# A two-layer transformer block: the first experts in two token batches, the second batch routed inside the experts' stage

## The chip, the core and the metric

One core of a Trainium2 chip. Its engines run side by side, each with its own instruction stream, and meet only through semaphores: PE (matmul, with PEld for its weight loads), DVE (elementwise and reductions), ACT (activation functions), POOL (elementwise, and the indirect DMAs that send and gather rows) and SP (which does nothing but read registers and issue DMAs). The metric is the device time of one execution in microseconds (us). Before the change its median of three runs is 1006.11 us (1004.85 to 1008.36).

## The reference

x is (128, 64, 128) in fp32: 8192 tokens of 128 values, here 64 tiles of 128 tokens, or 32 groups of two tiles. Four sublayers follow one another, each added to x after a layer norm:

```python
x = x + cross_attention_0(norm(x), ctx, ctx, padding)   # 16 heads of 8, causal, exact softmax
x = x + moe_0(norm(x))                                  # 16 experts, top 2
x = x + cross_attention_1(norm(x), ctx)                 # 2 heads of 64
x = x + moe_1(norm(x))                                  # 8 experts, top 1, and a shared expert
```

The sublayer that the change turns about is moe_0. Written as the kernel computes it, with xt the normed tokens:

```python
logits = xt @ Wr + br                       # 16 logits a token
w, idx = top_k(softmax(logits), 2); w /= w.sum()
h = gelu(xt @ W1[e] + b1[e])                # 128 -> 256, for the token's two experts e
y = xt + sum(w[e] * (h @ W2[e] + b2[e]) for e in idx)
```

Here the sublayer itself adds xt (the normed rows) as well.

## The kernel before

The program is a row of stages, each a block in which every engine has its own program; a stage begins when all engines have ended the one before. The stages are `opening`, `layer0_attention`, `experts` (with gated=False), `layer1_attention`, `route_and_share` and `experts` again (gated=True). x stays in SBUF (`x_sb` in the trace) from the beginning to the end.

`opening` (L67) loads x in four quarters on SP (L94), the small weights on ACT's queue, and behind x, on SP too, eight later loads (L96): the weights of the second attention and of the routers. The first attention begins when SP has issued them.

`layer0_attention` (L205) works in steps i, one group of two tiles a step: scores, softmax over four large DVE operations (L389 is the first of them), transposes, output, sum into x (L419). SP loads the context of each group (L276) into two buffers. Three steps behind (LATE = 3) the group is normed a second time (L377, into `f_xn_all`), transposed (L648), and multiplied with the router (L671); DVE keeps the logits (L412), finds the best two (`best_of`, L1194), and for chunks of 8 tiles (at the end, of 4) chooses and counts: matmuls give every token its rank within its expert (L1162, L1164), and `places` turns ranks to row numbers. POOL then sends each tile's rows to their experts' regions in DRAM, two indirect DMAs a tile (`send`, L1155). So steps 0 to 31 do attention, steps 3 to 34 routing, and the tail finishes the last chunks. SP loads, after the last context, 32 pieces of expert weights (L1117, L1120), then writes zeros: one spare region (L1138), 15 spare pieces of the output (L1141), and, when the counts are known, behind each expert's last row one block (`blank_rows`, L1132; SP takes eight experts and ACT eight; four row numbers at a time are read into registers). DVE computes from the counts which slot works on which expert and rows (`starts`, then `slots_by_partition` and `outs_by_partition`), PE turns that table (L686), and DVE keeps it.

`experts` (L1474) walks 80 slots: 64 pairs of 256 rows and 16 singles of 128 rows. In slot J SP loads the rows (L1540, four buffers, the row number from a register; a table of four is read at a time), PE transposes them (L1677), ACT copies, PE multiplies with W1 (L1694), ACT applies gelu (L1664), PE multiplies with W2 (L1704), DVE adds the bias (L1614, the slot's result) and copies the weights of the expert two slots ahead (L1587). POOL stores the result (L1560), again from a table of row numbers, and beside it sums x with the normed rows (L1563), 32 times in all. In the singles DVE also computes from where each token's two results are to be fetched (L1624 to L1630). PE's order in a slot is turn(J + 1), W1 of J, W2 of J - 1; PE works its instructions in order.

`layer1_attention` (L690) lets POOL gather for each tile the two result rows of each token (L758, 128 indirect DMAs in all, into a ring of buffers), DVE weights and adds them to x (L771), norms (L796), and PE begins with L948. PE, ACT and DVE walk the groups in hardware loops.

Of the kernel before, what the change touches and what calls it, by code (L numbers as in the profile page):

```python
# [37 lines left out]
X_CHUNKS = 4  # L38

# [27 lines left out]
def opening(nc, A, R):  # L67
    n = TILES // X_CHUNKS
    with ExitStack() as ctx:
# [4 lines left out]
        R.later_loaded = sem("later_loaded")  # L74
# [9 lines left out]
        for tag, (wr, br) in R.router.items():  # L84
            later += [(wr[:, :], A[tag + "_wr"]), (br[:, :], A[tag + "_br"].partition_broadcast(P))]
        R.later = len(later)
# [118 lines left out]
def layer0_attention(nc, A, R, N):  # L205

    NT, NG, E = TILES, GROUPS, N.experts
    CHUNKS = [8] * 6 + [4] * 4
# [3 lines left out]
    RANKED = [i + 2 if i < NG else i + 1 for i in CHOOSES]  # L212
    PLACES = [i + 1 if i < NG else i for i in RANKED]
    LAST = NG + LATE
    assert FIRST[-1] == NT
# [10 lines left out]
    with ExitStack() as ctx:  # L226
# [4 lines left out]
        ctxT = sb("ctxT", [P, 2, GT])  # L231
# [7 lines left out]
        K = Ranks(nc, ctx, A, R, N, max(CHUNKS))  # L239
# [19 lines left out]
        st0_done, slots_done, table_ready = sem("st0_done"), sem("slots_done"), sem("table_ready")  # L259
        xn_ready, xb_done, xk_done, xnT_ready, kx_ready = (sem(n) for n in ("xn_ready", "xb_done", "xk_done", "xnT_ready", "kx_ready"))  # L260
# [10 lines left out]
        def _(sp):  # L271
# [13 lines left out]
            K.clear_tails(sp, R.zeros[:, :, :], N.experts // 2)  # L285

        @block.gpsimd
        def _(pool):
# [31 lines left out]
            def body(p, k, low):  # L320
# [3 lines left out]
                if k == 1 and low >= 1 and within(i - LATE, NG):  # L324
                    inverse(p - 1)

            LAST_INVERSE, sent = NG + 1, 0
            for i in range(LAST_INVERSE + 1):
                placed = [FIRST[c + 1] for c in range(len(CHUNKS)) if PLACES[c] < i]
                tiles = min(2 if i < 24 else 3, max(placed, default=0) - sent)  # L330
                if i == LAST_INVERSE:
                    at_hand = max(FIRST[c + 1] for c in range(len(CHUNKS)) if PLACES[c] < NG)
                    for t in range(sent, at_hand + 1):
                        K.send(pool, max(c for c in range(len(CHUNKS)) if FIRST[c] <= t), t, t + 1)
                    sent, tiles = at_hand + 1, 0
                if i <= LAST_INVERSE:
                    body(i // 2, i % 2, i // 2)
                for n, t in enumerate(range(sent, sent + tiles)):
                    if n < 2 and within(i, NG):
                        pool.wait_ge(mx_done, 2 * i + n + 1)  # L340
                    K.send(pool, max(c for c in range(len(CHUNKS)) if FIRST[c] <= t), t, t + 1)
                sent += tiles
            for t in range(sent, TILES):
                K.send(pool, max(c for c in range(len(CHUNKS)) if FIRST[c] <= t), t, t + 1)
            pool.wait_ge(K.sent, 16 * TILES * N.top)

        @block.vector
        def _(dve):
# [84 lines left out]
            def body(p, k, low):  # L433
                i = 2 * p + k
                scored, added = within(i, NG), within(i - 1, NG)
                routed = 2 * low + k >= LATE and within(i - LATE, NG)
                if within(i + 2, NG):
                    norm(i + 2)
                if within(i - 2, NG):
                    statistics(i - 2, k)  # L440
# [7 lines left out]
                if routed and i <= NG + 1:  # L448
                    second_norm(i - LATE, p - 2 + k, k)
                if i == NG + 1:  # L450
                    second_norm(NG - 1, p - 1, 0)
# [5 lines left out]
                if LATE < i <= NG + LATE:  # L457
# [5 lines left out]
                for c in range(len(CHUNKS)):  # L463
                    if PLACES[c] == i != RANKED[c]:
                        K.places(dve, c, FIRST[c], CHUNKS[c])
                    if PLACES[c] == i == RANKED[c] and added:
                        K.positions(dve, rank_ps, c, FIRST[c], CHUNKS[c])
# [4 lines left out]
                for c in range(len(CHUNKS)):  # L472
                    if PLACES[c] != i == RANKED[c]:
                        K.read_ranks(dve, rank_ps, c, CHUNKS[c])
                    if PLACES[c] == i == RANKED[c] and not added:
                        K.positions(dve, rank_ps, c, FIRST[c], CHUNKS[c])
            passes(body)
            K.starts(dve)
            K.slots_by_partition(dve)
            K.outs_by_partition(dve)  # L480
            dve.sem_inc(slots_done, 1)
# [4 lines left out]
        def _(act):  # L486
# [39 lines left out]
            def body(p, k, low):  # L526
                i = 2 * p + k
                routed = 2 * low + k >= LATE and within(i - LATE, NG)
# [26 lines left out]
        def _(pe):  # L555
            def proj_xk(G, g, use):
                pe.wait_ge(loaded[g], 16 * (use + 1))
# [35 lines left out]
            def turn(i, u):  # L593

                pe.wait_ge(p_ready, 2 * i + u + 1)
                for half in range(2):
                    if u == 0 and half == 0 and needed(i - LATE + 1):
# [9 lines left out]
            def weighted(i, u, g):  # L607
# [3 lines left out]
                if u == 0 and needed(i + 1 - LATE):  # L611
# [15 lines left out]
            def body(p, k, low):  # L627
                i = 2 * p + k
                r = i - LATE
                routed = 2 * low + k >= LATE and within(r, NG)  # L630
                if within(i, NG):
                    scores(i, k)
                if i - 1 in RANKED and not within(i - 1, NG):
                    pe.wait_ge(K.read, RANKED.index(i - 1) + 1)
# [22 lines left out]
                if routed:  # L657
# [8 lines left out]
                    else:  # L666
                        pe.wait_ge(x_done, NG)
                    if i in RANKED and i in PLACES and within(i - 1, NG):
# [375 lines left out]

# [768 lines left out]
```

## Time and profile before

| | us |
|---|---|
| median of 3 runs | 1006.11 (1004.85 to 1008.36) |
| the profiled execution | 1005.86 |
| its span in the trace | 1004.0 |
| PE busy in the span | 821.1 (82%) |
| DVE busy | 666.0 (66%) |
| ACT busy | 578.2 (58%) |
| POOL busy | 511.1 (51%) |
| opening until the next stage's first instruction | 17.16 |
| first transpose of the experts | 400.44 |
| last result of the experts | 550.26 |
| first matmul of the second attention | 573.29 |

A busy share is the mean over stages that have different limits, so it is read by stage: the windows view gives for a stretch the busy time of each engine, the granted clock of TensorE as a share of full speed (PEclk) and the DMA engines' share. In a timeline, the brackets behind a row hold the idle time of its engine before it and the instruction that released it. SPq, POOLq, PEq and so on are the queues of the engines (DMA issues and signals); "issue" means that nothing in the trace explains the wait.

### The profile page before, as it was taken

How to read it: one execution, taken by the hardware profiler on the slowest of the kernel's cores; microseconds unless marked ns; L12 is line 12 of the kernel's file. 1: busy time of each engine (PE TensorE's matmuls, PEld its weight loads, DVE VectorE, ACT ScalarE, POOL GpSimd, SP SyncE). 2: the span in 40 equal slices, each digit the busy share in tenths (PEclk: the TensorE clock that was granted, in tenths of full speed). 3: DMA queues.
4: the chain of work that ended last, by engine and by line, in shares of the span. 5: the costliest groups of instructions: out<-in, count | busy, mean ns of one | idle time of the engine just before them, and what ended most of it. 6: DMA issues, size and time to landing. Idle time of an engine off the chain costs nothing. (4 is left out here: it accounts for less than half of the span.)

```text
span 1004.0 us, 27974 instructions
## 1 busy us (share of the span) xinstructions
PE 821.1 (82%) x9234; PEld 689.1 (69%) x9234; DVE 666.0 (66%) x2294; ACT 578.2 (58%) x1339; POOL 511.1 (51%) x612
## 2 busy tenths in 40 slices
PE   0699999999999820999998178888858998959997
PEld 0478877878777710999997055555547887849996
DVE  3788899999989742344446379999963546425554
ACT  0588888888888500666665177777756551213332
POOL 4011145555564765344445677777400644726777
PEclk9799999999999855999999599999998999979999
DMA  6000011111116413344332233333213213244441
GB/s 206 11 19 18 14 39 37 47 44 40 49 40 194 143 45 101 112 135 136 131 125 94 72 83 78 82 82 79 55 31 124 85 67 118 107 137 141 145 122 55
DMA packets 67572, 86.33 MB, mean 86 GB/s; under 512 B 22000, under 2 KB 50037, under 8 KB 66960
## 3 DMA queue, kind: packets, MB, share of 16 engines
q1 hardware_dynamic: 47728, 44.71, 15.2%
q0 software_dynamic: 17152, 39.36, 12.1%
q10 hardware_dynamic: 2592, 0.95, 0.5%
q8 instruction: 60, 0.98, 0.4%
q14 instruction: 40, 0.33, 0.1%
HBM read 50.47 MB, written 35.01 MB: 85 GB/s over the span
## 5 line engine op out<-in xcount | busy, mean ns | idle before, releaser
L1155 POOL DMA_INDIRECT f_rows_in<-f_xn_all,f_pos_i x128 | 126.1, 985 | 68.5 <-DVE a_mx L389 34.4
L758 POOL DMA_INDIRECT a_got<-f_rows_out,f_pos_i x128 | 122.7, 958 | 41.5 <-issue 35.4
L1155 POOL DMA_INDIRECT f_rows_in<-f1r_xn_all,f_pos_i x64 | 61.6, 962 | 70.8 <-DVEq L1222 31.3
L1552 POOL DMA_INDIRECT out<-f1e_y,f1e_ids x72 | 76.5, 1062 | 41.3 <-DVE f1e_y L1611 24.7
L1560 POOL DMA_DIRECT2D f_rows_out<-f0e_y x80 | 43.8, 547 | 88.3 <-DVE f0e_y L1614 71.4
L1664 ACT ACTIVATE f0e_hT<-f0e_ps_h,f0e_w 128x256 f32<-128x256 f32 (+1 forms) x160 | 63.8, 449 | 38.5 <-PE f0e_ps_h L1694 38.5
L1614 DVE TENSOR_TENSOR f0e_y<-f0e_ps_y,f0e_w 128x256 f32<-128x256 f32 (+1 forms) x80 | 31.7, 397 | 80.9 <-PE f0e_ps_y L1704 80.6
L618 PE MATMUL a_ps_o<-vx,a_prT 128*64 128x18 f32 x2048 | 83.6, 215 | 2.0 <-DVE x_sb L419 2.0
L618 PEld LDWEIGHTS a_ps_o<-vx,a_prT 128*64 128x64 f32 x2048 | 79.7, 140 | 7.7 <-issue 4.7
L293 POOL TENSOR_TENSOR x_sb<-x_sb,bo 128x256 f32<-128x256 f32 x32 | 23.3, 727 | 116.3 <-DVE a_xn L354 116.0
L389 DVE TENSOR_REDUCE a_mx<-a_ps_s 128x16 f32<-128x1024 f32 x64 | 77.7, 1215 | 5.1 <-PE a_ps_s L589 4.9
L512 ACT ACTIVATE a_pr<-a_pr,sharp 128x1024 f32<-128x1024 f32 x64 | 74.1, 1158 | 10.0 <-DVE a_pr L397 9.4
L1694 PE MATMUL f0e_ps_h<-f0e_xT,f0e_w 128*128 128x256 f32 (+1 forms) x320 | 77.9, 367 | 2.2 <-ACT f0e_xT L1646 1.8
L397 DVE TENSOR_TENSOR a_pr<-a_ps_s,a_mx 128x1024 f32<-128x1024 f32 x64 | 77.9, 1216 | 1.7
L604 PE MATMUL a_ps_t<-ident,a_pr 128*128 128x128 f32 x512 | 71.4, 281 | 9.0 <-ACT a_xnT L542 5.3
L1704 PEld LDWEIGHTS f0e_ps_y<-f0e_w,f0e_hT 128*128 128x128 f32 x576 | 76.0, 192 | 3.8 <-ACT f0e_hT L1664 0.4
L1704 PE MATMUL f0e_ps_y<-f0e_w,f0e_hT 128*128 128x128 f32 x576 | 77.8, 276 | 0.2 <-ACT f0e_hT L1664 0.2
L519 ACT ACTIVATE a_prT<-a_ps_t 128x512 f32<-128x512 f32 x128 | 69.4, 594 | 14.6 <-PE a_ps_t L604 14.4
L604 PEld LDWEIGHTS a_ps_t<-ident,a_pr 128*128 128x128 f32 x512 | 55.4, 142 | 29.1 <-issue 14.1
L1694 PE MATMUL f1e_ps_h<-f1e_xT,f1e_w 128*128 128x256 f32 (+1 forms) x320 | 70.2, 363 | 0.1
L490 ACT ACTIVATE a_kx<-a_ps_p,own_bk,own 128x256 f32<-128x256 f32 x128 | 65.8, 577 | 0.0
L1601 DVE TENSOR_TENSOR f1e_hT<-f1e_ps_h,f1e_hg 128x512 f32<-128x512 f32 (+1 forms) x40 | 25.5, 638 | 50.3 <-ACT f1e_hg L1659 41.9
(300 smaller groups left out, 2043.3 us busy)
## 6 DMA issues: line engine op xcount, KB each, us to landing
f1e_x<-f_rows_in SPq DMA_DIRECT2D x32, 272.0 KB, 2.7
a_ctxT<-in_ctxT SPq DMA_DIRECT2D x64, 128.0 KB, 2.1
f0e_x<-f_rows_in SPq DMA_DIRECT2D x64, 128.0 KB, 2.0
f_rows_out<-f0e_y POOLq DMA_DIRECT2D x64, 128.0 KB, 2.0
f_w<-in_f_w SPq DMA_DIRECT2D x16, 257.0 KB
x_sb<-in_x SPq DMA_DIRECT2D x4, 1024.0 KB, 5.0
f_w<-in_f_w SPq DMA_DIRECT2D x8, 384.0 KB, 6.4
f_rows_in<-f_xn_all,f_pos_i POOLq DMA_INDIRECT x128
```

Source lines behind the costliest of these rows:

```text
L389: dve.tensor_reduce(by_strip(mx[:, u, :]), scores(u), AX.X, ALU.max).then_inc(mx_done, 1)
L397: dve.tensor_tensor(pr[:, u, :, :].rearrange("p (s j) k -> p s j k", s=STRIPS), scores(u), peaks, ALU.subtract).then_inc(d_ready, 1)
L490: last = act.activation(kx[:, g, j, :], ps_p[:, GT:2 * GT], ACT.Identity, scale=R.own[:, j:j + 1], bias=R.own_bk[:, j:j + 1])
L512: act.activation(pr[:, u, :, :], pr[:, u, :, :], ACT.Exp, scale=R.sharp[:, bass.ds(2 * i + u, 1)]).then_inc(p_ready, 1)
L519: act.activation(prT[:, u, js, :], ps_t[:, js, :], ACT.Copy).then_inc(t_evac, 1)
L604: last = pe.transpose(ps_t[:, j, :], pr[:, u, 2 * j:2 * j + 2, :].rearrange("p h k -> p (h k)"), ident[:, :])
L618: last = pe.matmul(ps_o[rows, 144 * u + 18 * j:144 * u + 18 * j + 18], prT[:, u, j, rows], vx[:, g, 2 * u + b, j, :, :].rearrange("p e c - ...
L758: pool.indirect_dma_start(got[:, n, k, :], None, N.rows_out[0:N.most, :], bass.IndirectOffsetOnAxis(ap=N.pos_i[:, k, t:t + 1], axis=0)).th ...
L1155: pool.indirect_dma_start(N.rows_in, bass.IndirectOffsetOnAxis(ap=N.pos_i[:, k, t:t + 1], axis=0), self.xn_all[:, t, :], None).then_inc(se ...
L1552: pool.indirect_dma_start(rows_of_out, bass.IndirectOffsetOnAxis(ap=ids[:, n, u:u + 1], axis=0), y[:, n, u, :], None, bounds_check=B * S - ...
L1694: last = pe.matmul(ps_h[m][:, j, 0:size], w[:, n, j * P:(j + 1) * P], xT[:, m, 0:size], start=True, stop=True)
L1704: last = pe.matmul(ps_y[1 - m][:, u * P:(u + 1) * P], hT[:, 1 - m, j, u * P:(u + 1) * P], w[:, l, H + j * C:H + (j + 1) * C], start=(j == ...
```

## The change

The tokens are routed in two batches, tiles 0 to 47 and tiles 48 to 63, each with its own rows in DRAM, its own counts and its own slots.

- Opening: SP issues the context of groups 0 and 1 behind the first quarter of x, and the eight later loads move into the first attention's SP program, behind the loads of its first two groups there.
- First attention: only groups 0 to 23 are routed, in six chunks of 8 tiles; the blocks, starts and slots are computed in steps 30 to 32. POOL sends 48 tiles. SP writes the spare zeros of both batches (2 x 16 pieces) before the tail blanks.
- First experts: a stage of its own, `first_experts`, with all loops unrolled, for 64 slots of batch A (48 pairs, 16 singles) and 32 of batch B (16 pairs, 16 singles): 96 in all. SP issues both the loads and, six slots behind, the stores of the results. Groups 24 to 31 are normed, transposed and given logits in slots 11 to 20, chosen and ranked in 22 to 29, and their table is made in 31 to 41; POOL sends their rows. At slot 46 SP blanks batch B's sixteen tails. POOL first does the sums of x, then, after the sends and when all of A's results are stored, gathers the first 18 tiles for the second attention.
- Second attention: POOL gathers from tile 18 on, into a ring of 16 groups that lies where the normed rows were; DVE's loop is unrolled.
- The second experts keep their work, as `second_experts`.

```diff
@@ opening, SP
                 if c == 1:
+                    for g in range(2):
+                        sp.dma_start(R.ctxT[:, g, :], A["ctxT"][:, GT * g:GT * (g + 1)]).then_inc(R.ctx_first[g], 16)
                     sp.wait_ge(w_loaded, 16 * len(first))
                 sp.dma_start(R.x[:, tiles, :], R.xd[:, tiles, :]).then_inc(R.x_loaded[c], 16)
-            for place, data in later:
-                sp.dma_start(place, data).then_inc(R.later_loaded, 16)
@@ layer0_attention
-    CHUNKS = [8] * 6 + [4] * 4
+    EG = EARLY // 2
+    CHUNKS = [8] * (EARLY // 8)
-    LAST = NG + LATE
+    LAST = NG
@@ layer0_attention, SP
-            rounds(sp, body, NG // 2, last=0)
+            for place, data in R.later_loads:
+                sp.dma_start(place, data).then_inc(R.later_loaded, 16)
+            body(1)
+            with sp.Fori(2, NG // 2) as i:
+                body(i)
             K.load_weights(sp, shared=False)
             sp.wait_ge(R.later_loaded, 16 * R.later)
             sp.wait_ge(zeros_made, 1)
+            spares = sum(blank_spare(sp, N, batch, R.zeros[:, :, :], spare_blank) for batch in N.batches)
             K.clear_tails(sp, R.zeros[:, :, :], N.experts // 2)
+            sp.wait_ge(spare_blank, 16 * spares)
@@ first_experts, SP
+            for J in range(NS + LAG):
+                if J == BLANK_AT:
+                    K.clear_tails(sp, R.zeros[:, :, :], E)
+                if J == NA:
+                    sp.wait_ge(slots_kept, 1)
+                    sp.wait_ge(K.sent, 16 * 2 * BG * N.top)
+                if J < NS:
+                    Q, j = batch(J)
+                    if j % NB == 0:
+                        rows = table(Q.slot_row[0:1, j:j + NB], mybir.EngineType.SP, Q.spare)
+                    if J >= NB:
+                        sp.wait_ge(xT_done, J - NB + 1)
+                    sp.dma_start(x[:, J % NB, 0:wide(J), :],
+                                 Q.rows_in[bass.ds(rows[j % NB], wide(J) * P), :].rearrange("(p u) c -> p u c", p=P)).then_inc(loaded[J % NB], 16)
+                if J >= LAG:
+                    L = J - LAG
+                    Q, j = batch(L)
+                    if j % NB == 0:
+                        outs = table(Q.slot_out[0:1, j:j + NB], mybir.EngineType.SP, Q.last_out)
+                    sp.wait_ge(y_ready, L + 1)
+                    sp.dma_start(Q.rows_out[bass.ds(outs[j % NB], wide(L) * P), :].rearrange("(p u) c -> p u c", p=P),
+                                 y[:, L % NB, 0:wide(L), :]).then_inc(stored[L % NB], 16)
@@ first_experts, POOL
+            for G in range(EARLY // 2):
+                sum_norm(G)
+            pool.wait_ge(ag_done, 1)
+            pool.tensor_scalar(var[:, :], mv[:, :, 1], EPS, None, ALU.add).then_inc(var_ready, 1)
...
+            pool.tensor_tensor(rstd[:, :], var[:, :], half[:, :], ALU.pow).then_inc(rstd_ready, 1)
+            for v in range(BG):
+                pool.wait_ge(K.kept, v + 1)
+                sum_norm(EARLY // 2 + v)
+            for t in range(EARLY, TILES):
+                K.send(pool, 0, t, t + 1)
+            pool.wait_ge(K.sent, 16 * 2 * BG * N.top)
...
+            for n in range(NB):
+                pool.wait_ge(stored[n], 16 * (NA // NB))
+            for t in range(FETCHED):
+                gather(pool, N, t)
@@ first_experts, DVE, for each J
+                    result(J - 1)
...
+                    weights(ahead, e[j % NB])
...
+                if NORM_AT <= J < NORM_AT + BG:
+                    norm(J - NORM_AT)
+                if LOGITS_AT < J <= LOGITS_AT + BG:
+                    keep_logits(J - LOGITS_AT - 1)
@@ first_experts, PE, for each J, behind turn(J + 1), W1 of J and W2 of J - 1
+                if TURN_AT <= J < TURN_AT + BG:
+                    v = J - TURN_AT
+                    pe.wait_ge(K.kept, v + 1)
+                    if v > 0:
+                        pe.wait_ge(nT_ready, v)
+                    for u in range(2):
+                        last = pe.transpose(ps_n[:, u * P:(u + 1) * P], N.xn_all[:, EARLY + 2 * v + u, :], R.ident[:, :])
+                    last.then_inc(nT_done, 1)
+                if LOGITS_AT <= J < LOGITS_AT + BG:
+                    v = J - LOGITS_AT
+                    pe.wait_ge(nT_ready, v + 1)
+                    if v > 0:
+                        pe.wait_ge(l_ready, v)
+                    for u in range(2):
+                        last = pe.matmul(l_ps[:, u, :], late_T[:, u * P:(u + 1) * P], wr[:, :], start=True, stop=True)
+                    last.then_inc(l_done, 1)
+                if J == RANK_AT:
+                    K.rank_matmuls(pe, rank_ps, 0, LATER)
@@ layer1_attention
-        got = sb("got", [P, 2 * NB, K, C])
+        got = N.xn_all[:, :, :].rearrange("p (n k) c -> p n k c", k=K)
```

The constants of the new stage are EARLY = 48, FETCHED = 18, RING = 16, LAG = 6, NORM_AT = 11, TURN_AT = 12, LOGITS_AT = 13, BEST_AT = 22, RANK_AT = 27, READ_AT = 28, BLOCKS_AT = 31, TABLE_AT = 37, TURNED_AT = 40, KEPT_AT = 41 and BLANK_AT = 46; NB = 4 buffers each for x, w and y.

## Rows read from the trace of the kernel before

**Rows 1.** Windows of three stages: seam, pairs, second attention (start:end, length, busy, granted clock).

```profile
354.00:400.00 46.00, 5.60 (x29) 3.59 (x28) 17.45 (x104) 0.77 (x2) 29.37 (x32) 0.50 0.23 69
...
400.00:531.00 131.00, 130.41 (x906) 122.77 (x907) 56.39 (x130) 80.77 (x198) 57.73 (x94) 0.98 0.40 128
...
573.00:749.00 176.00, 140.29 (x1472) 97.77 (x1472) 148.42 (x617) 124.66 (x380) 108.49 (x114) 0.98 0.27 67
```

**Rows 2.** Timeline of the opening (start, duration, engine, line, operation, idle before and its releaser).

```profile
12.47 0.61 SPq L96 DMA_DIRECT2D w1wq<-in_a_wq  x1
...
16.20 0.49 SPq L96 DMA_DIRECT2D f_br<-in_f_br  x1
...
17.21 1.86 DVE L354 TENSOR_SCALAR a_xn<-x_sb,mean,rstd 128x128 f32<-128x128 f32 x1 [4.40 <-PEq L69]
...
23.10 0.47 PE L562 MATMUL a_ps_p<-ident,a_xn 128*128 128x128 f32 x1 [10.89 <-DMA a_ctxT<-in_ctxT]
```

**Rows 3.** Timeline of DVE: the first reduction of four steps of the first attention.

```profile
57.27 1.23 DVE L389 TENSOR_REDUCE a_mx<-a_ps_s 128x16 f32<-128x1024 f32 x1 [0.42 <-PE a_ps_s L589]
...
65.95 1.22 DVE L389 TENSOR_REDUCE a_mx<-a_ps_s 128x16 f32<-128x1024 f32 x1 [0.42 <-PE a_ps_s L589]
...
287.05 1.21 DVE L389 TENSOR_REDUCE a_mx<-a_ps_s 128x16 f32<-128x1024 f32 x1
...
334.41 1.21 DVE L389 TENSOR_REDUCE a_mx<-a_ps_s 128x16 f32<-128x1024 f32 x1
```

**Rows 4.** Timeline around the end of the first attention: SP's queue, POOL, PE.

```profile
310.41 0.33 SPq L276 DMA_DIRECT2D a_ctxT<-in_ctxT  x1
...
329.10 10.20 SPq L1141 DMA_DIRECT2D f_rows_out<-zeros  x15
...
379.07 0.33 SPq L1132 DMA_DIRECT2D f_rows_in<-zeros  x1
...
381.27 1.88 SPq L1132 DMA_DIRECT2D f_rows_in<-zeros  x4
...
394.14 0.96 POOL L1155 DMA_INDIRECT f_rows_in<-f_xn_all,f_pos_i  x1 [0.30 <-issue]
...
400.44 0.48 PE L1677 MATMUL f0e_ps_x<-ident,f0e_x 128*128 128x128 f32 x1 [16.16 <-DMA f0e_x<-f_rows_in]
```

**Rows 5.** Timeline of DVE in the experts: first pair, last pair, last single.

```profile
407.03 0.42 DVE L1614 TENSOR_TENSOR f0e_y<-f0e_ps_y,f0e_w 128x256 f32<-128x256 f32 x1 [6.43 <-PE f0e_ps_y L1704]
407.37 0.48 DVE L1587 COPY f0e_w<-f_w 128x642 f32 x1
...
531.16 0.43 DVE L1614 TENSOR_TENSOR f0e_y<-f0e_ps_y,f0e_w 128x256 f32<-128x256 f32 x1 [0.61 <-PE f0e_ps_y L1704]
...
550.26 0.29 DVE L1614 TENSOR_TENSOR f0e_y<-f0e_ps_y,f0e_w 128x128 f32<-128x128 f32 x1 [0.60 <-PE f0e_ps_y L1704]
```

**Rows 6.** The page's DMA issues (out<-in, queue, count, KB each, us to landing).

```profile
f0e_x<-f_rows_in SPq DMA_DIRECT2D x64, 128.0 KB, 2.0
```

**Rows 7.** Routing's operations by line (count: ns min/median/max, first and last start).

```profile
L648 PE MATMUL a_ps_t<-ident,f_xn_all x64: 272/273/477, 70.2 to 368.9; 128*128 128x128 f32 x64
...
L671 PE MATMUL a_ps_o<-f_wr,a_xnT x128: 182/262/395, 72.0 to 370.4; 128*128 128x16 f32 x128
...
L377 DVE TENSOR_SCALAR f_xn_all<-x_sb,a_mv,a_rstd x64: 329/341/568, 69.2 to 365.2; 128x128 f32<-128x128 f32 x64
```

**Rows 8.** POOL's sums in the experts and its powers in the first attention, by line.

```profile
L1563 POOL TENSOR_TENSOR x_sb<-x_sb,f_xn_all x32: 737/744/913, 410.7 to 532.8; - x28, 128x256 f32<-128x256 f32 x4
...
L302 POOL TENSOR_TENSOR a_rstd<-a_var,minus_half x16: 1037/1042/1048, 68.1 to 363.4; 128x4 f32<-128x4 f32 x16
```

**Rows 9.** The gathers of the second attention, who waited for them, and its first matmul.

```profile
L758 POOL DMA_INDIRECT a_got<-f_rows_out,f_pos_i x128: 940/947/1168, 554.6 to 715.0; - x128
...
  DVE x_sb L771: 9.7, 6
...
573.29 0.45 PE L948 MATMUL a_xk<-ident,a_xn 128*128 128x128 f32 x1 [23.07 <-DVE a_xn L796]
```

More of the change, by code:

```diff
@@ L38 @@
 X_CHUNKS = 4
+EARLY = 48
+FETCHED = 18
+RING = 16
 def needed(count):
@@ L462, in body @@
                     K.choose(dve, FIRST[c], CHUNKS[c])
[L463 to L467, printed above, removed]
+                if i in PLACES:
+                    c = PLACES.index(i)
+                    K.places(dve, c, FIRST[c], CHUNKS[c])
+                if i == NG - 2:
+                    K.blocks_by_expert(dve)
+                if i == NG - 1:
+                    K.starts(dve)
                 if added:
@@ L471, in body @@
                     keep_logits(i - LATE)
[L472 to L476, printed above, removed]
+                if i in RANKED:
+                    c = RANKED.index(i)
+                    K.read_ranks(dve, rank_ps, c, CHUNKS[c])
             passes(body)
[L478 to L481, printed above, removed]
             dve.wait_ge(table_ready, 1)
@@ L1040, in clear_stale, with __init__ @@
     R.stale = []
[L1043 to L1062 removed]
+class Batch:
+    def __init__(self, nc, sb, N, tag, first, tiles):
+        self.first, self.tiles, experts = first, tiles, N.experts
+        self.region = tiles * P + SLOT
+        self.pairs, self.singles = tiles * P * N.top // SLOT, experts
+        self.slots = self.pairs + self.singles
+        self.spare = experts * self.region
+        self.rows_in = nc.dram_tensor(f"{tag}_rows_in", (self.spare + SLOT, N.row), F32, kind="Internal").ap()
+        self.slot_e = sb(tag + "_slot_e", [P, LEAD + self.slots], I32)
+        self.slot_row = sb(tag + "_slot_row", [P, self.slots], I32)
+        if not N.final:
             self.sure, self.most = 2 * self.pairs * P, (2 * self.pairs + experts - 1) * P
@@ L1243, in starts @@
              dve.scalar_tensor_tensor(self.until[:, :], own[:, 0, :], float(SLOT), start[:, :], ALU.mult, ALU.add))
+    def starts(self, dve):
+        E, N, Q = self.N.experts, self.N, self.Q
+        step = lambda *instructions: self.step(dve, *instructions)
+        start, own, ends = self.start, self.own, self.ends
         a, b, d = own, self.sums, 1
@@ L1289, in keep_slots, with blank_spare @@
     def keep_slots(self, dve, turned):
-        N = self.N
-        dve.tensor_copy(N.slot_e[0:1, LEAD:], turned[:, 0:N.slots])
-        dve.tensor_copy(N.slot_row[0:1, :], turned[:, P:P + N.slots])
-        if not N.final:
-            dve.tensor_copy(N.slot_out[0:1, :], turned[:, 2 * P:2 * P + N.slots])
+        Q = self.Q
+        if not self.N.final:
+            dve.tensor_copy(Q.slot_out[0:1, :], turned[:, 2 * P:2 * P + Q.slots])
+        dve.tensor_copy(Q.slot_row[0:1, :], turned[:, P:P + Q.slots])
+        return dve.tensor_copy(Q.slot_e[0:1, LEAD:], turned[:, 0:Q.slots])
+def blank_spare(queue, N, Q, blank, done):
+    queue.dma_start(Q.rows_in[Q.spare:, :].rearrange("(p u) c -> p u c", p=P), blank).then_inc(done, 16)
+    if N.final:
+        return 1
+    for row in range(Q.sure, Q.most, P):
+        queue.dma_start(Q.rows_out[row:row + P, :], blank[:, 0, :]).then_inc(done, 16)
+    return 1 + (Q.most - Q.sure) // P
 def route_and_share(nc, A, R, N):
@@ L1534, in body @@
             def body(i):
-                rows = table(N.slot_row[0:1, bass.ds(NB * i, NB)], NB, mybir.EngineType.SP, N.spare)
+                rows = table(Q.slot_row[0:1, bass.ds(NB * i, NB)], NB, mybir.EngineType.SP, Q.spare)
                 for n in range(NB):
```

539 lines of the change are left out of this document (348 added, 191 removed).

## The prediction

> **What bounds the kernel now.** I read the stage windows first, then the waits, then the timelines at the seams between stages. The first experts run on a full PE: busy 130.4 of 131 us [rows 1]. The seam before them is nearly empty: of 46 us PE works 5.6 and DVE 17.5 [rows 1]. The change buys time at three seams (opening, routing tail, start of the second attention) and pays for it inside the stage that has no idle PE. So there are two columns: what the seams give, and what the experts' stage grows by.
>
> The profiled execution took 1005.86 us (span 1004.0, the rest lies around it), 0.25 below the median of 1006.11, so what I take off or add to one holds for the other.
>
> **A, opening: -7.7.** The next stage starts at 17.21 with a norm, because SP still issues its eight later loads, the first at 12.47, the last at 16.20 [rows 2]. PE then starts at 23.10, released by the context DMA, which queues behind x [rows 2]. With both edits the stage starts when DVE's opening ends, about 13.3 (some 0.5 after SP's x loads are issued, 12.47). The first norm takes 1.86 us [rows 2], so PE starts near 15.3, 7.8 earlier; I count 7.7 for a slightly late quarter of x. The eight loads still cost SP about 4.2 us, now beside a step of about 8.7; nobody waits for them before the blanking, and SP has done its context loads of that step. Bounds: 0 (if what is late next is the rest of x, whose statistics DVE takes right behind) and 9.
>
> **B and C, the end of the first attention: together with A -47.** A step with no routing lasts 65.95 - 57.27 = 8.68; the last five average (334.41 - 287.05)/5 = 9.47 [rows 3]. Routing now ends with group 23, three steps late, so five steps lose 0.8 each. Then the tail: today POOL's last send ends at 394.14 + 0.96 = 395.10 and the experts' first transpose is at 400.44, 5.3 later [rows 4]. With 96 sends, up to three tiles a step, the sends end a few us after the last step begins (334.41 - 7.7 - 4.0 = 322.7), near 340. So what is late next? SP. Its program is: last context load (310.41 today; less 7.7 and two shortened steps, 301.1); 32 weight loads and the first spare blank, after which it stands at 329.10 today, 18.7 later, so at 319.8; then the other spare blanks, 15 today in 10.20 us, 0.68 each [rows 4], 31 now, 21.1: 340.9. Then eight tail blanks behind two register tables: a blank every 0.52 (four in 1.88), a table between 379.07 and 381.27 adds 2.20 - 0.52 = 1.68 [rows 4], so 8 x 0.52 + 2 x 1.68 = 7.5: 348.4. Plus the same 5.3 for landing, barrier and first load: 353.7 instead of 400.44, -47. Bounds: -53 if the spare blanks go at 0.5 each, -40 if the sends or the last output set the end.
>
> **D, 96 slots for 80, and SP carries stores: +28.** A pair takes (531.16 - 407.03)/63 = 1.97 us, a single (550.26 - 531.16)/16 = 1.19 [rows 5]. Sixteen more singles at that rate: +19. But SP now issues a load and a store per slot and reads two register tables per four slots: 8 x 0.52 + 2 x 1.68 = 7.5 by the rows of the blanking; where a table's read lies partly beside a wait, less (I estimate down to 1.1 a table, 6.4). I take 7.0 for four slots, 1.74 a slot. That hides under a pair (1.97), not under a single. SP starts a run of singles about four or five slots ahead and needs one or two for the landing of 2.0 us [rows 6]; with 2.5 slots to use up, n singles go at 1.19 until 1.19 n = 1.74 (n - 2.5), n = 8. So 8 x 1.19 + 8 x 1.74 = 23.5 for each sixteen, twice 47, less 19.1 = +28. Bounds +19 (SP hidden) and +36 (no lead). *The Trainium skill's page DMA: Bandwidth & Descriptors (Issuing engines are not separate DMA queues) holds that issuing from several engines saves only sequencer time, which is usually small beside the DMA. By that, giving the stores to SP costs nothing, D is +19 and the sum 1017; the rows of SP show why I don't follow it here: issue and table together are near the length of a slot.*
>
> **E, routing's PE work: +9.** Eight times two transposes (0.273 each) and four logit records (0.262 each) [rows 7] are 1.6 us end to end, about half where they overlap: 6.4 to 12.8. With 17 or more rank records of that kind and the slot table, 9 (7 to 16). PE has no idle time in the pairs, so this is on the path.
>
> **F, waits that routing adds: +25.** In slots 14 to 20 PE's logits of group v wait for DVE's reading of group v-1, since both use one piece of PSUM, and DVE reads only after that slot's result: y_done, result 0.42, weights 0.48 [rows 5], the norms of two tiles at 0.341 each [rows 7], then the reading itself, a smaller operation than the result; some 0.2 with its signals, my estimate. That is 1.7 us in which PE holds its next slot's matmuls behind the logits in order. 7 x 1.65, and one or two of these slots also hold DVE's register table: 13.6. The norm at slot 11 waits for POOL: 24 sums of 0.744 are 17.9 us, then a power over 128x16 [rows 8], which the trace shows only at 128x4, 1.04 us: between 1.04 and 4.2, I take 2. Slot 11 comes at about 23 us (cold first slots, row 407.03 is 6.6 after the first transpose), so this costs 0 to 6, I take 3. Choosing, ranks and reading (slots 22 to 28) are a round trip DVE, PE, DVE of some ten short operations, and PE's rank matmuls stand in order behind the choice; starts and slots (29 to 41) are longer chains of such operations, with only the slot table waited for by PE. DVE's lead of two slots, 3.9 us, hides what is shorter than that: between 0 and 12 for all, and I take 8.5, nearer the upper end, since the logits' slots have used up that lead. Bounds for F: +8 (only one short wait in each logits slot) and +32.
>
> **G, blanking at slot 46: +15.** SP stops its loads and stores for 16 blanks and four tables, 16 x 0.52 + 4 x 1.68 = 15.0, waits for them to land (2.0) and then loads slot 46, which takes 0.5 and 2.0 [rows 4, 6]: 19.5. It begins when SP is four slots ahead of PE, worth 4 x 1.97 = 7.9 less what SP waits for that slot's result, about 7. PE stands 12.4; the results stand too, because stores of slots 40 to 43 are behind the blanks and y has four buffers. Today's stage also shows the granted clock at 0.50 after an empty stretch [rows 1]; a pause of 12 us can cost 2 to 3 more. Bounds: +6 (lead of six slots and faster blanks) and +18.
>
> The stage grows by 28 + 9 + 25 + 15 = **+77**.
>
> **H, second attention: -9.4.** Its first matmul is at 573.29 after 23.07 idle; DVE waited 9.7 us in six waits for gathers issued from 554.55 on, (715.0 - 554.6)/127 = 1.26 us apart [rows 9]. 18 tiles (36 gathers, 45 us) now go beside batch B's slots (16 x 1.97 + 23.5 = 55 us), after all of A's stores, and so end in time. Later gathers: 4 x 1.26 = 5.0 per group of two tiles, against 176/32 = 5.5 for a group of this stage [rows 1], with nine groups of lead: not late. Bounds 0 and -10. DVE's unrolled loop and the second experts: 0, between -2 and +2.
>
> **Sum:** 1005.9 - 47 + 77 - 9.4 = 1026.5; forecast **1026 us, slower**. Its own range is 1012 to 1042, from the bounds of F, G and D taken together.
>
> **Rivals.**
> *PE stays fed (other side).* Four x and y buffers and a lead of two slots cover the logits round trips and most of the blanking. Then only D and E are left, +28 to +37, and F and G give 0 to 12: 1005.9 - 47 + 37 - 9.4 = 986, range 970 to 1003. For it: DVE is busy for 0.42 + 0.48 of each 1.97 in the pairs [rows 5], and a small operation finds room. Against: PE works in order, and the logits stand between two slots' matmuls. It decides where F and G together stay below 19.4 of my 40.
> *SP bounds all slots.* If an issue with its waits takes 0.6 and a table 1.7, a slot is 2.05 for pairs too: 64 x 0.08 + 16 x 0.3 = +10 on the sum, 1036. Against: 64 slots have a slack of 0.2.
> *Half clock inside the stage.* The stretch 354 to 400 had 0.50 [rows 1]. If the thinned slots 11 to 28 or those after the blanking run at 1.2 GHz, some 10 us of PE work count twice: 1038.
> *The early gathers come late.* If B's slots pass faster than 45 us, or gathers wait for A's last stores, H is lost: 1035. Here the change would not do what it says at that seam.
> *Nothing measurable.* F and G at half: 1006.
>
> **How the numbers follow.** Forecast 0.42, PE fed 0.24, SP 0.09, clock 0.10, late gathers 0.08, no difference 0.07. A run of this kernel tells about 3 us (0.3%) from nothing. So faster 0.24, same 0.07, slower 0.69. Range **985 to 1042**: half of the fast rival and the top of the clock's lie outside.
>
> **What would show it.** The first transpose of the experts near 353.7, with SP's blanks as the last releaser (if POOL's sends or the last output are, C's steps are wrong). PE idle before the logits' line in seven slots, released by DVE; one idle of some 12 us before the transpose of slot 46, released by DMA. Results of the later singles 1.7 apart. The second attention's first matmul some 13 us after the experts' last result, not 22.7. If the stage from first transpose to last result is below 206 us instead of 227, I am wrong on the sign, and the idle times before these two lines say which of F and G it was.

## The result: 3.5% slower, and the profile after

The changed kernel takes 1042.45 us (median of four runs, 1037.80 to 1045.56) against 1005.48 for the kernel before on the same chip; the ratio is 1.0349, with a 95% interval of 1.0315 to 1.0383. The forecast was slower, 1026, in a range of 985 to 1042, so the median lies just above its upper end. The sign was right; some 15 us of the experts' stage were missing from the sum.

The profiled execution is the fastest of the four (1037.80, span 1036.0), so the terms below add up to +32 of the median's +37. The other three, which left no trace, show a mean granted clock of 0.935 to 0.946 against 0.952, and their 5 us stay open.

The windows of the changed kernel, with the columns of [rows 1]: the seam behind the last output of the first attention, then A's pairs, A's singles, B's pairs, B's singles.

```profile
339.00:349.30 10.30, 0.81 (x4) 0.22 (x2) 1.45 (x5) 0.00 (x0) 2.65 (x5) 0.50 0.45 120
349.30:502.00 152.70, 115.87 (x751) 104.72 (x752) 66.58 (x268) 63.18 (x157) 56.15 (x63) 0.92 0.34 103
502.00:529.80 27.80, 19.25 (x149) 17.14 (x149) 14.63 (x39) 14.10 (x48) 0.00 (x0) 1.00 0.30 85
529.80:565.60 35.80, 31.84 (x224) 29.48 (x223) 14.80 (x38) 19.34 (x49) 23.25 (x23) 1.00 0.55 156
565.60:591.20 25.60, 20.07 (x138) 18.79 (x136) 10.61 (x31) 12.69 (x44) 12.86 (x13) 0.87 0.41 111
```

The seam of 46 us [rows 1] is 10 us now. In return PE, which was busy in 130.4 of 131 us, stands for 37 of the 153 us of A's pairs.

The granted clock of TensorE has a smaller part in it. In the stage of before it is at full speed (2.4 GHz) from 406.5 on; here it falls to half (1.2 GHz) six times behind the first slots. The first four lines are from A's pairs, the last two from B's singles:

```profile
390.30:393.70 3.40, 2.87 (x13) 2.33 (x11) 0.92 (x3) 0.93 (x3) 0.00 (x0) 0.51 0.14 39
434.80:438.20 3.40, 3.24 (x21) 2.92 (x22) 0.84 (x3) 0.38 (x1) 0.00 (x0) 0.51 0.18 60
448.40:451.80 3.40, 3.40 (x15) 3.13 (x14) 1.58 (x11) 1.12 (x3) 2.48 (x4) 0.50 0.53 163
485.40:495.70 10.30, 5.11 (x18) 4.64 (x19) 0.83 (x2) 1.60 (x4) 0.25 (x1) 0.53 0.34 100
571.20:574.50 3.30, 3.30 (x18) 3.30 (x18) 1.15 (x4) 1.77 (x6) 2.62 (x3) 0.51 0.50 134
584.90:588.40 3.50, 3.50 (x19) 3.50 (x18) 1.07 (x5) 1.60 (x6) 0.00 (x0) 0.51 0.30 84
```

PE is busy for 21.4 us in them. Four W1 products take 1.92 us at half clock (491.07, shown under e4) and 1.03 at full clock, so I estimate that about half of the 21.4 is due to the clock: some 7 us in A's pairs and 3 in B's singles. Each fall comes during or soon after a wait of PE, but other waits (3.39 us until 409.05) bring none, and no run changes the clock alone.

The timelines of the changed kernel at the places of [rows 2], [rows 4] and [rows 9]: PE's first matmul, SP's and ACT's last blanks, the experts' first transpose and last result, the second attention's first matmul.

```profile
14.88 0.66 PE L570 MATMUL a_ps_p<-ident,a_xn 128*128 128x128 f32 x2 [3.08 <-DVE a_xn L361]
...
327.79 8.37 SPq L1305 DMA_DIRECT2D f0b_rows_out<-zeros  x15
337.96 5.47 SPq L1137 DMA_DIRECT2D f0b_rows_in<-zeros  x8
338.48 5.29 ACTq L1137 DMA_DIRECT2D f0b_rows_in<-zeros  x8
349.36 0.48 PE L1748 MATMUL f0e_ps_x<-ident,f0e_x 128*128 128x128 f32 x1 [9.55 <-DMA f0e_x<-f0b_rows_in]
...
591.17 0.29 DVE L1618 TENSOR_TENSOR f0e_y<-f0e_ps_y,f0e_w 128x128 f32<-128x128 f32 x1 [0.60 <-PE f0e_ps_y L1756]
603.57 0.66 PE L951 MATMUL a_xk<-ident,a_xn 128*128 128x128 f32 x2 [12.44 <-DVE a_xn L800]
```

| part | forecast | measured on the profiled execution |
|---|---|---|
| A, B, C: first transpose of the experts | -47 | 349.36 - 400.44 = -51.1 |
| D to G: experts, first transpose to last result | +77 | (591.17 - 349.36) - (550.26 - 400.44) = +92.0 |
| H: last result to the next first matmul | -9.4 | 12.40 - 23.03 = -10.6 |
| the rest | 0 | (1036.0 - 603.57) - (1004.0 - 573.29) = +1.7 |
| sum | +20.6 | +32.0 |

So three of the four rows came out within some 4 us, and the stage's row is the one that was missed. What PE waited for in that stage, as the waits view of the changed kernel groups it (total, times, longest):

```profile
PE f0e_ps_x L1748 <- DMA f0e_x<-f0b_rows_in: 25.7, 9, 9.5
PE f0e_ps_h L1772 <- issue: 13.1, 8, 2.4
PE f0e_ps_r L1793 <- DVE f0r_logits L1643: 12.8, 7, 3.4
PE f0e_ps_h L1772 <- ACT f0e_xT L1720: 9.5, 11, 1.2
PE f0e_ps_r L1159 <- DVE f0r_chosen L1201: 3.0, 1, 3.0
```

Three of these were forecast: the seven waits for logits (L1793), the wait for ranks (L1159), and the blanking, which is 8.9 of the first line (another 9.5 of it is the stage's start, and 7.3 are waits for the rows of singles). The two lines of L1772, PE's first product with W1, were not: nineteen waits and 22.6 us, of which 12.1 fall in A's pairs, 4.0 in B's pairs and 6.6 in the singles. The profile names ACT's xT or nothing at all for them. DVE's and PE's timelines in one such slot show what is behind it:

```profile
356.75 0.42 DVE L1618 TENSOR_TENSOR f0e_y<-f0e_ps_y,f0e_w 128x256 f32<-128x256 f32 x1 [0.27 <-PE f0e_ps_y L1756]
359.09 0.66 DVE L1609 COPY f0e_w<-f_w 128x642 f32 x1 [1.92 <-PE f0e_ps_y L1756]
...
359.85 1.10 PE L1772 MATMUL f0e_ps_h<-f0e_xT,f0e_w 128*128 128x256 f32 x4 [0.95 <-ACT f0e_xT L1720]
```

The matmul starts 0.10 after the copy of its weights ends (359.09 + 0.66 = 359.75); ACT had been done since 358.94 + 0.38 = 359.32. And the copy starts 1.92 after the result, though in other slots it follows at once [rows 5]. Between the two DVE reads the numbers of the next four experts into registers; such instructions are not counted as busy, so no row shows them. In the code of before this read stands at the head of the four slots, ahead of the wait for the first result; in the change it stands behind the result.

### The profile page after: what moved, and what is told of

Its sections match the earlier page's. It is cut to its first block and busy times, and to the rows that moved or that the text cites. A ratio compares the mean times of both kernels' runs of the same rounds, so it can differ in the third digit from the quotient of the medians.

```text
span 1036.0 us, 27913 instructions
## 1 busy us (share of the span) xinstructions
PE 851.1 (82%) x9381; PEld 713.7 (69%) x9381; DVE 679.4 (66%) x2352; ACT 590.8 (57%) x1387; POOL 466.7 (45%) x526
## 5 line engine op out<-in xcount | busy, mean ns | idle before, releaser
L1152 POOL DMA_INDIRECT f0b_rows_in<-f_xn_all,f_pos_i x128 | 125.9, 983 | 103.2 <-DVE a_mx L396 37.2
L694 POOL DMA_INDIRECT f_xn_all<-f0b_rows_out,f_got_i x128 | 124.1, 970 | 100.8 <-DMA f0b_rows_out<-f0e_y 49.8
L1731 ACT ACTIVATE f0e_hT<-f0e_ps_h,f0e_w 128x256 f32<-128x256 f32 (+1 forms) x192 | 73.6, 434 | 66.7 <-PE f0e_ps_h L1772 66.5
L1772 PE MATMUL f0e_ps_h<-f0e_xT,f0e_w 128*128 128x256 f32 (+1 forms) x384 | 92.4, 366 | 22.6 <-issue 13.1
L1878 POOL DMA_INDIRECT out<-f1e_y,f1e_ids x72 | 76.6, 1064 | 42.7 <-DVE f1e_y L1917 27.6
L1152 POOL DMA_INDIRECT f1b_rows_in<-f1r_xn_all,f_pos_i x64 | 61.4, 959 | 71.2 <-DVEq L1219 31.5
L1756 PE MATMUL f0e_ps_y<-f0e_w,f0e_hT 128*128 128x128 f32 x640 | 91.5, 284 | 0.2 <-ACT f0e_hT L1731 0.2
L1756 PEld LDWEIGHTS f0e_ps_y<-f0e_w,f0e_hT 128*128 128x128 f32 x640 | 88.3, 200 | 4.0 <-ACT f0e_hT L1731 0.4
L1772 PEld LDWEIGHTS f0e_ps_h<-f0e_xT,f0e_w 128*128 128x128 f32 x384 | 64.4, 203 | 30.7 <-issue 14.7
L1609 DVE COPY f0e_w<-f_w 128x642 f32 x96 | 50.2, 525 | 53.2 <-issue 36.7
L1720 ACT ACTIVATE f0e_xT<-f0e_ps_x 128x256 f32<-128x256 f32 (+1 forms) x96 | 33.4, 348 | 58.0 <-PE f0e_ps_x L1748 57.5
```

What stands on the lines that cost most here:

```text
L694: pool.indirect_dma_start(N.xn_all[:, N.top * place + k, :], None, Q.rows_out[0:Q.most, :], bass.IndirectOffsetOnAxis(ap=N.got_i[:, k, t:t ...
L1152: pool.indirect_dma_start(Q.rows_in, bass.IndirectOffsetOnAxis(ap=N.pos_i[:, k, t:t + 1], axis=0), self.xn_all[:, t, :], None).then_inc(se ...
L1731: last = act.activation(hT[:, m, j, 0:size], ps_h[m][:, j, 0:size], ACT.Gelu, bias=w[:, J % NB, B1 + j:B1 + j + 1])
L1756: last = pe.matmul(ps_y[m][:, u * P:(u + 1) * P], hT[:, m, j, u * P:(u + 1) * P], w[:, n, H + j * C:H + (j + 1) * C], start=(j == 0), stop ...
L1772: last = pe.matmul(ps_h[m][:, j, 0:size], w[:, n, j * P:(j + 1) * P], xT[:, m, 0:size], start=True, stop=True)
L1878: pool.indirect_dma_start(rows_of_out, bass.IndirectOffsetOnAxis(ap=ids[:, n, u:u + 1], axis=0), y[:, n, u, :], None, bounds_check=B * S - ...
```

## The experiments

Each ran against the kernel before; "less" and "more" are differences of ratios, times 1006. The changed kernel is at 1.0349. Most ratios are known to 0.002 or 0.003 either way, so a difference of two of them to some 4 us.

**e1, the opening alone** (kernel before, with only the edits of the opening).

```diff
+                    for g in range(2):
+                        sp.dma_start(R.ctxT[:, g, :], A["ctxT"][:, GT * g:GT * (g + 1)]).then_inc(R.ctx_first[g], 16)
...
-            for place, data in later:          # in opening; now in layer0_attention, behind its first loads
...
```

> The kernel before with the opening's two edits alone (context of groups 0 and 1 behind the first quarter of x, the eight later loads in the next stage). My theory (term A): everything behind the opening moves up with the first matmul, -7 to -9 us, about 997.5. Rival: only the first matmul moves, and the statistics that DVE takes of the last quarter of x hold the first step, so 0 to -3 us.

0.9911 (0.9889 to 0.9934), 999.24 us: 9 us less than before. Its first matmul is at 15.24 instead of 23.10 [rows 2], and its first softmax reduction at 30.17 instead of 38.0. Term A holds, and x's last quarter does not delay the first step.

**e2, the register table ahead of the result.**

```diff
             for J in range(-LEAD, NS + 1):
-                if 0 < J:
-                    result(J - 1)
                 ahead = J + LEAD
                 if ahead < NS:
...
                     if j % NB == 0:
                         e = table(Q.slot_e[0:1, LEAD + j:LEAD + j + NB], mybir.EngineType.DVE, E - 1)
+                if 0 < J:
+                    result(J - 1)
+                if ahead < NS:
                     weights(ahead, e[j % NB])
```

> The changed kernel, with DVE reading its register table of the next four experts ahead of the slot's result (while it waits for PE anyway) instead of behind it. Theory: the idle times of PE before its first W1 matmul, 1.0 to 2.7 us in every fourth slot, are this table, which stands between the result and the copy of the next weights: 14.6 us in batch A's pairs, 4 more in the two logit slots that hold a table, and some 5 to 11 in batch B and the singles, so -15 to -25 us, about 1020. Rival: these waits are the fetching of the unrolled program or a busy SBUF port; then the order of the two changes nothing, 1038 to 1045.

1.0195 (1.0165 to 1.0225): 15.5 us less than the changed kernel. DVE's timeline of e2 at a slot with a table:

```profile
365.41 0.42 DVE L1618 TENSOR_TENSOR f0e_y<-f0e_ps_y,f0e_w 128x256 f32<-128x256 f32 x1 [0.70 <-PE f0e_ps_y L1757]
365.75 0.48 DVE L1609 COPY f0e_w<-f_w 128x642 f32 x1
```

The copy follows the result at once, and the waits of PE at its W1 product fall from 22.6 to 9.2 in e2. The place of the table was the cause, not the fetching of the unrolled program. Of the 9.2, 8.6 are four waits that stay, in slots 11, 31, 35 and 39 (7.6 in the changed kernel). There DVE comes late from its routing work and has no wait in which the read could hide; its idle time now stands before the result:

```profile
436.32 0.17 DVE L1218 CAST f_pos_i<-f_pos 128x16 int32<-128x16 f32 x1
438.82 0.42 DVE L1618 TENSOR_TENSOR f0e_y<-f0e_ps_y,f0e_w 128x256 f32<-128x256 f32 x1 [2.33 <-issue]
```

**e10, the same order in the kernel before.** The opposite test: only the place of this read is changed, in the hardware loop of before.

```diff
-                if ahead > 0:
+                if gated and ahead > 0:
                     e = table(N.slot_e[...], ahead, mybir.EngineType.DVE, N.experts - 1)
...
+                    if n == 0 and not gated and ahead > 0:      # behind the result of slot J - 1
+                        e = table(N.slot_e[...], ahead, mybir.EngineType.DVE, N.experts - 1)
                     if within(J + LEAD, NS):
                         weights(J + LEAD, (n + LEAD) % NB, e[n])
```

> The kernel before with one thing changed: in its first experts DVE reads the register table of the next four experts behind the slot's result instead of ahead of it (the order that the change has). Theory: the wait found in the changed kernel comes from this order alone and shows up here too, some 1.0 us in each of the 16 pair tables and about 1.2 in four single tables: +13 to +22 us, about 1023. Rival: it comes from the change's other load on DVE and SP, and here the two slots of lead hide it: within 4 us.

1.0187 (1.0165 to 1.0209), 1026.28 us: 19 more than before, from twenty tables, 0.9 a table, and the same rows:

```profile
429.63 0.42 DVE L1614 TENSOR_TENSOR f0e_y<-f0e_ps_y,f0e_w 128x256 f32<-128x256 f32 x1 [1.25 <-PE f0e_ps_y L1706]
431.60 0.77 DVE L1587 COPY f0e_w<-f_w 128x642 f32 x1 [1.54 <-PE f0e_ps_y L1706]
```

Neither batches nor unrolling are needed for this loss; the order of two steps is enough.

**e3, logits kept once.** Each late group has its own columns, PE does not wait for DVE between groups, and DVE keeps all eight in one operation.

```diff
-        l_ps = ps_r[:, 0:2 * E].rearrange("p (t e) -> p t e", e=E)
+        l_ps = ps_r[:, 0:LATER * E].rearrange("p (t e) -> p t e", e=E)
...
-                    if v > 0:
-                        pe.wait_ge(l_ready, v)
...
-                if LOGITS_AT < J <= LOGITS_AT + BG:
-                    keep_logits(J - LOGITS_AT - 1)
+                if J == LOGITS_AT + BG:
+                    keep_logits()
```

> The changed kernel, with the logits of the eight late groups in columns of their own in PSUM and kept by DVE in one operation after the last, so that PE no longer waits for DVE between two groups. Theory (term F): seven idle times of PE before the logits, 14.8 us in all, go, less the two register tables among them that stay (some 2 us each): -10 to -14 us, about 1030. Rival: PE then waits as long for ACT's copy of the transposed rows in the same slots, and less than 4 us are gained.

1.0188 (1.0160 to 1.0215): 16.2 less, above the -10 to -14 expected. (The seven waits are 12.8 us by the waits view, not 14.8.) One reason is that the two slots with a register table lost most of their wait as well: slot 14 takes 3.25 us instead of 7.31, slot 18 3.25 instead of 6.22. Slots 15 to 17 took 4.23 us each in the changed kernel; slots 16 and 17 take 2.59 here, which is 1.97 [rows 5] and the late group's own matmuls. The rows of PE there, in e3, follow without idle time:

```profile
391.49 0.38 PE L1785 MATMUL f0e_ps_n<-ident,f_xn_all 128*128 128x128 f32 x2
391.71 0.52 PE L1791 MATMUL f0e_ps_r<-f_wr,f0e_late_T 128*128 128x16 f32 x4
```

**e4, blanks one a slot, on ACT.**

```diff
-                if J == BLANK_AT:
-                    K.clear_tails(sp, R.zeros[:, :, :], E)
...
+                if BLANKS <= J < BLANKS + E:      # ACT; BLANKS = 32, a table before every fourth
...
+                    act.dma_start(QB.rows_in[bass.ds(rows[b % 4], P), :], R.zeros[:, 0, :]).then_inc(K.cleared, 16)
```

> The changed kernel, with batch B's sixteen tails blanked from ACT's queue, one in each of slots 32 to 47 (a register table before every fourth), instead of all at once by SP ahead of slot 46. Theory (term G): the idle time of 9.1 us before slot 46's transpose and the stretch at a lower clock behind it go: -10 to -14 us, about 1030. Rival: ACT's 16 issues of 0.5 and four tables delay its gelu and give most of it back: -5 us or less.

1.0210 (1.0180 to 1.0240): 14.0 less. In the changed kernel PE stood for 8.9 us and came back with matmuls at half the speed (four W1 products in 1.92 us, against 1.03 in e4):

```profile
480.68 1.05 PE L1756 MATMUL f0e_ps_y<-f0e_w,f0e_hT 128*128 128x128 f32 x8
490.59 0.69 PE L1748 MATMUL f0e_ps_x<-ident,f0e_x 128*128 128x128 f32 x2 [8.86 <-DMA f0e_x<-f0b_rows_in]
491.07 1.92 PE L1772 MATMUL f0e_ps_h<-f0e_xT,f0e_w 128*128 128x256 f32 x4
```

e4 has the same three lines without a gap, at full speed:

```profile
481.37 1.05 PE L1762 MATMUL f0e_ps_y<-f0e_w,f0e_hT 128*128 128x128 f32 x8
482.26 0.38 PE L1754 MATMUL f0e_ps_x<-ident,f0e_x 128*128 128x128 f32 x2
482.48 1.03 PE L1778 MATMUL f0e_ps_h<-f0e_xT,f0e_w 128*128 128x256 f32 x4
```

**e5, e2 to e4 together.**

> The changed kernel with the three edits of e2, e3 and e4 together (register table ahead of the result, logits kept once, blanks on ACT one a slot). Theory: the three waits are separate, so their gains of about 15.5, 16 and 14 us add up, 1042 - 45 = 995 to 1000, faster than the kernel before. Rival: they cover for each other (SP's stores and loads become the bound once PE waits less), and the sum stops at -25 to -30, about 1014.

0.9977 (0.9958 to 0.9996), 1005.32 us: 37.4 less than the changed kernel where the three alone sum to 45.7. Some 4 us are counted twice, the tables in two of the logits' slots, which e2 and e3 both remove. A's singles take 29.5 us in e5 and 27.1 in e4: they don't get shorter when PE waits less elsewhere, and 6.8 us of them run at half clock in e5. The other 2 us are within the intervals.

**e6, e5 with the last singles' stores on POOL.**

```diff
+            for L in range(52, 64):               # POOL; SP leaves these out
+                if L % NB == 0:
+                    outs = table(QA.slot_out[0:1, L:L + NB], mybir.EngineType.Pool, QA.last_out)
+                pool.wait_ge(y_ready, L + 1)
+                pool.dma_start(QA.rows_out[bass.ds(outs[L % NB], wide(L) * P), :]..., y[:, L % NB, 0:wide(L), :])
```

> As e5, and the stores of the last twelve singles of batch A (slots 52 to 63) issued by POOL, which is idle there, instead of SP. Theory (term D): SP's issues and register tables, 7.0 us per four slots, set the pace of these singles (1.7 us a slot); with the stores gone it is 1.0 to 1.4: -4 to -8 us against e5. Rival: DVE's table and copies set it as well, and less than 2 us are gained.

0.9921 (0.9893 to 0.9949): 5.6 less than e5, and A's singles take 23.9 us instead of 29.5. SP was their bound. Part of the gain is clock: e6 shows no stretch at half clock in these singles, and e4, which shows none there either and leaves the stores on SP, takes 27.1. SP's queue in the changed kernel, in the middle of them, alternates between loads and stores without rest, and stops only for a table:

```profile
518.57 0.33 SPq L1569 DMA_DIRECT2D f0b_rows_out<-f0e_y  x1
519.08 0.35 SPq L1561 DMA_DIRECT2D f0e_x<-f0b_rows_in  x1
521.00 0.33 SPq L1569 DMA_DIRECT2D f0b_rows_out<-f0e_y  x1
521.52 0.52 SPq L1561 DMA_DIRECT2D f0e_x<-f0b_rows_in  x1
```

**e7, no early gathers.** One constant: FETCHED = 0 for 18.

> The changed kernel without the early gathers (none of the 18 tiles beside batch B's slots; all 128 gathers in the second attention as before). Theory (term H): its first matmul comes 9 to 11 us later and the rest follows, so +8 to +11 us over the changed kernel, about 1052. Rival: the second attention waits later for what it lacks now, so that the difference is under 4 us; or the gathers beside the slots hold up batch B's loads, and leaving them out gains inside the experts what it loses behind.

1.0415 (1.0379 to 1.0452): 6.6 more by the medians, while the two intervals just overlap (1.0383 and 1.0379). The seam itself is clear. Its trace has the last result at 593.29 and the second attention's first matmul here, 22.8 later, as in the kernel before:

```profile
616.06 0.66 PE L951 MATMUL a_xk<-ident,a_xn 128*128 128x128 f32 x2 [22.80 <-DVE a_xn L800]
```

**e8, batch B's spare blanks on POOL, and e9, e8 and e6 together.**

```diff
-            spares = sum(blank_spare(sp, N, batch, R.zeros[:, :, :], spare_blank) for batch in N.batches)
+            spares = blank_spare(sp, N, N.batches[0], R.zeros[:, :, :], spare_blank)
...
+            blank_spare(pool, N, QB, R.zeros[:, :, :], spare_blank)      # first_experts, ahead of the sends
```

> The changed kernel, with the 16 spare blanks of batch B issued by POOL in the experts' stage, ahead of its sends, instead of by SP in the first attention. Theory (term C): SP's row of blanks is what ends the first attention, and 8.8 us of it go, until the slot table (DVE, 340.3) is the last: the experts start 4 to 5 us earlier; POOL's 10 us of blanks lie in a wait of 35 us for the places: -3 to -5 us. Rival: POOL's sends or the last output end the stage anyway: within 1 us, or later sends cost what is gained.

> e6 and e8 together: the changed kernel with the register table ahead of the result, logits kept once, blanks on ACT, stores of the last singles of batch A on POOL, and batch B's spare blanks on POOL. Theory: e6's 1000.4 less the 4 us that e8 gained at the end of the first attention: 995 to 998, faster than the kernel before by about 1%. Rival: POOL's added blanks push its sends back, now that the slots run faster, and batch B's loads wait for the sends: 999 to 1003.

e8 is at 1.0309 (1.0282 to 1.0335), 4.0 less than the changed kernel by the medians, with intervals that overlap; e9 is at 0.9923 (0.9901 to 0.9945), no better than e6. Both traces refute my theory, so e8's 4 us, if they are real, are not from this seam: SP's last blanks go out at 333 to 336, but the experts' first transpose does not move (e8, then e9).

```profile
349.06 0.48 PE L1750 MATMUL f0e_ps_x<-ident,f0e_x 128*128 128x128 f32 x1 [9.41 <-DMA f0e_x<-f0b_rows_in]
```

```profile
348.86 0.47 PE L1773 MATMUL f0e_ps_x<-ident,f0e_x 128*128 128x128 f32 x1 [9.11 <-DMA f0e_x<-f0b_rows_in]
```

POOL's sends were hardly pushed back either: the last one is at 467.7 in e9 and 467.6 in e6, and 2.3 later in e8 than in the changed kernel. What stayed is ACT's row of eight blanks; in e8 it is issued from 338.38 on for 5.13 us:

```profile
336.62 0.38 ACT L550 ACTIVATE a_aoT<-a_ps_t 128x256 f32<-128x256 f32 x1 [5.93 <-PE a_ps_t L659]
338.38 5.13 ACTq L1137 DMA_DIRECT2D f0b_rows_in<-zeros  x8
```

**e11, e9 with all of batch A's tails on SP.**

```diff
-            K.clear_tails(sp, R.zeros[:, :, :], N.experts // 2)
+            K.clear_tails(sp, R.zeros[:, :, :], N.experts)
...
-            K.blank_rows(act, mybir.EngineType.Activation, R.zeros[:, :, :], N.experts // 2, N.experts)
```

> e9, and all sixteen tails of batch A blanked by SP, none by ACT. e8 and e9 left the experts' first transpose at 349, though SP's own blanks were out by 334 to 336; the shared semaphore of the tails came at 344.7. Theory: ACT's eight blanks, issued from some 337 on, behind its last work in the attention, end the stage together with SP's, so that only taking both away moves it: SP would be done near 341, the first transpose comes 2 to 4 us earlier, near 346, and the time falls to 997 to 999. Rival: the landing of POOL's last sends or the slot table holds the stage to 348 or later, and nothing is gained.

The first transpose moves to where the theory had it, 2.3 earlier than in e9:

```profile
346.52 0.47 PE L1772 MATMUL f0e_ps_x<-ident,f0e_x 128*128 128x128 f32 x1 [6.91 <-DMA f0e_x<-f0b_rows_in]
```

The time is 998.19 us, 0.9912 (0.9893 to 0.9931). By the medians it is the fastest version with two batches, though not clear of e6 and e9, and it is faster than both kernels. But the opening alone (e1) stands at 0.9911: with every wait repaired that was found, the two batches give nothing measurable beyond what the opening gives by itself.

## Why the forecast had the sign right and the size short

- **A** (-7.7): right. First matmul 14.88 (forecast 15.3), and e1 confirms it alone.
- **B and C** (with A -47): right in size, -51.1, and half right in the cause. SP's blanks end at 337.96 + 5.47 = 343.4, forecast 348.4, since the spare ones took 0.56 each (8.37 for 15) and not 0.68; but ACT's end at 338.48 + 5.29 = 343.8, and both count into the same semaphore. My list of what is late next had SP, the sends and the last output, and not ACT, whose blanks stand behind its own last attention work. e8 and e11 tell the two apart.
- **D** (+28): the singles take (529.74 - 502.02) + (591.17 - 565.61) = 53.3 us, 34.2 more than the 19.1 of before. That SP paces A's singles is shown by e6. Of the 6 us above the forecast, table and clock are about 1: e2, with the read moved and no half clock in the singles, still takes 27.6 for A's instead of 27.7 and 24.5 for B's instead of 25.6. The rest is mostly A's: their 27.7 is 16 x 1.74, so the 2.5 slots that SP was to be ahead did not show. In B's singles PE waits 5.4 us for rows in e2, which points to SP there too; no run takes their stores off SP.
- **E** (+9): the late matmuls cost 2.59 - 1.97 = 0.6 a group in e3, near the forecast's 0.8 for overlapped records; rank and table were not measured alone. The remainder of the sum below leaves 9.6 for all of E.
- **F** (+25): right in size, 23.4. The logits' waits are 12.8 us in seven slots (forecast 11.6 and a table's 2). Choosing, ranks, starts and slots are 3.0 (L1159) and 7.6 (the W1 waits of slots 11, 31, 35 and 39), against 8.5 and the 3 for the norm at slot 11, where no wait for POOL shows.
- **Missing: DVE's register table.** The step F says that "one or two of these slots also hold" it, as if it cost only there. I took the tables of all other slots as hidden, because they are hidden in the trace of before, and did not look at which side of the result the new loop reads them. Beside the slots of F and the singles they show as 4.5 us of W1 waits in A's pairs and 4.0 in B's. Reading them ahead of the result gains more, 15.5 (e2), among other things since the waits for logits lose 3.8 with it; that this is just 92 - 77 is chance.
- **G** (+15): about 11.5. PE stands 8.9 us at the blanking, not 12.4, and works 5.1 us at half clock behind it, of which half is put down to the clock; e4 gives 14.0, within the noise.
- **The sum of the stage.** D is 6.2 above the forecast, F 1.6 and G 3.5 below it; the tables beside F add 8.5 and the half clock in A's pairs beside the blanking some 4.8 (half of 9.5). With the 0.6 that are left for E these are the 15 us. So the sum lacked two terms, the tables and the clock outside the blanking, and the errors of the others partly cancelled.
- **H** (-9.4): -10.6 in the profile, and e7 returns 10.4 of it in its own; its medians give 6.6 with a wide interval.
- **Rivals.** PE did not stay fed. SP did not bound the pairs (1.97 where no table falls). The half clock did take part: by the estimate above some 7 us in A's pairs, 2.6 of them behind the blanking, where its rival had 10. It came on top of the waits. The gathers were not late.

## What to carry to other kernels

When a loop is rewritten, compare the order of its steps on each engine with the old loop, register reads included: an instruction that the busy rows don't show costs nothing ahead of a wait that is long enough to hold it, and up to its whole length behind that wait or where there is none (e2). When a bound is removed at the end of a stage, list every engine that counts into the semaphore the stage ends on. And test the cheap part of a change alone: here one small edit carried the whole gain.

## What was not expected of the hardware

A read of four numbers into registers, with the checks that go with it, holds an engine's program for 1.5 to 2 us: the copy starts 359.09 - (356.75 + 0.42) = 1.92 after the result in the changed kernel, where it otherwise follows at once, and 1.54 after it in e10. On SP the same shows as 521.00 - 519.08 = 1.92 between two issues that are otherwise 0.51 apart.
